# Cross-attention and feed-forward of a decoder layer as one block: one batch after the other, with the gate and up weights' codes transposed during the mixer

## The reference, cut to what matters

```python
x = x + mixer(layernorm(x))                       # scan over time, 2048 channels, 16 states, then @ W_out.T
x = x + matmul(fake_quant(layernorm(x), s1, z1), fake_quant(ctx, s2, z2))
def qlinear(x, w):                                # both sides: round(t / s) * s, s = max|row| / 127
    return einsum('bsh,oh->bso', fake_quant(x, -1), fake_quant(w, 1))
h = silu(qlinear(n, w_gate)) * qlinear(n, w_up)   # n = layernorm(x); 2752 hidden channels
x = x + qlinear(h, w_down)
```

## Time and profile before

| what | us |
|---|---|
| median of 3 runs | 1680.31 (1670.72 to 1685.57) |
| the profiled execution | 1669.6 |
| its span, first to last instruction | 1667.8 |
| PE busy | 1408.3 (84%) |
| DVE busy | 1335.1 (80%) |
| ACT busy | 929.3 (56%) |
| POOL busy | 946.3 (57%) |

### The profile page before, as it was taken

One profiled execution on the slowest core, in us unless ns is written; L12 is line 12 of the kernel. 1 busy time (PEld: TensorE's weight loads), 2 busy tenths in 40 slices (PEclk: granted clock), 3 DMA queues, 4 the chain that ended last, 5 costly groups with the idle time before them and its releaser, 6 DMA issues. The chain is left out here.

```text
span 1667.8 us, 17950 instructions
## 1 busy us (share of the span) xinstructions
PE 1408.3 (84%) x5576; PEld 727.8 (44%) x5576; DVE 1335.1 (80%) x1641; ACT 929.3 (56%) x1375; POOL 946.3 (57%) x767
## 2 busy tenths in 40 slices
PE   6999577788888987768898888888999994999898
PEld 3444344444444443444454454444434442444443
DVE  6585899999999979999999988889047556777684
ACT  1211557768768655867767767755234122556670
POOL 0000679889899878879999898897100000333300
PEclk9999788999999999877999999999999996999899
DMA  7597333443453432433683682664473103589504
GB/s 275 201 351 261 92 118 107 169 145 107 152 162 108 169 101 96 140 100 111 216 274 113 225 273 82 237 217 158 168 290 132 54 26 94 137 189 192 121 3 174
DMA packets 155468, 264.38 MB, mean 159 GB/s; under 512 B 76560, under 2 KB 94096, under 8 KB 149552
## 3 DMA queue, kind: packets, MB, share of 16 engines
q1 hardware_dynamic: 151056, 236.27, 43.9%
q10 hardware_dynamic: 4320, 27.00, 4.4%
HBM read 207.60 MB, written 38.60 MB: 148 GB/s over the span
## 5 line engine op out<-in xcount | busy, mean ns | idle before, releaser
L1093 DVE TENSOR_TENSOR_SCAN hbuf<-decay,hbuf 128x512 f32<-128x512 f32 x492 | 587.2, 1208 | 24.0 <-ACT decay L788 23.5
L788 ACT ACTIVATE decay<-delta,chan_sb 128x512 f32<-128x512 f32 x492 | 334.2, 686 | 281.9 <-DVE hbuf L1093 280.4
L598 PE MATMUL turn<-ident,hbuf 128*128 128x128 f32 x2048 | 338.2, 295 | 179.2 <-DVE hbuf L1093 128.7
L598 PEld LDWEIGHTS turn<-ident,hbuf 128*128 128x128 f32 x2048 | 255.1, 150 | 450.6 <-DVE hbuf L1093 199.6
L1107 DVE SCALAR_TENSOR_TENSOR acc<-turn,pn,acc 128x512 f32<-128x512 f32 x360 | 262.2, 728 | 41.1 <-PE turn L598 40.1
L927 POOL TENSOR_TENSOR hbuf<-wout,sx 128x512 f32<-128x512 f32 x172 | 216.0, 1289 | 15.0 <-DVE wout L1080 15.0
L927 POOL TENSOR_TENSOR hbuf<-du,sx 128x512 f32<-128x512 f32 x172 | 218.5, 1305 | 1.7 <-DMA sx<-bt_scratch 1.7
L948 POOL TENSOR_TENSOR acc<-acc,part 128x512 f32<-128x512 f32 x120 | 153.1, 1276 | 52.1 <-ACT part L798 51.0
L1796 PE MATMUL bank<-codes,wout 128*128 128x512 bf16 (+1 forms) x704 | 153.9, 382 | 1.0 <-PEq L1210 1.0
L580 PE MATMUL bank_g<-wout,codes 128*128 128x512 f32 x256 | 136.9, 622 | 0.0
L510 PE MATMUL bank_u<-wout 128*128 128x512 f32 x224 | 113.2, 625 | 3.7 <-DMA wout<-in_wu 2.8
(11 more groups left out here) (217 smaller groups left out, 2171.0 us busy)
## 6 DMA issues: line engine op xcount, KB each, us to landing
wout<-in_woutT SPq DMA_DIRECT2D x48, 512.0 KB, 4.2
sx<-bt_scratch SPq DMA_DIRECT2D x86, 256.0 KB, 3.7
codes<-in_wg SPq DMA_DIRECT2D x8, 2048.0 KB, 9.3
ubuf<-u_scratch SPq DMA_DIRECT2D x16, 1024.0 KB, 6.6
wout<-in_w_gate SPq DMA_DIRECT2D x26, 512.0 KB, 4.8
wout<-in_w_up SPq DMA_DIRECT2D x26, 512.0 KB, 4.6
raw_d<-in_w_down ACTq DMA_DIRECT2D x8, 1376.0 KB, 7.0
b_more<-bt_scratch SPq DMA_DIRECT2D x42, 256.0 KB, 3.5
```

The costliest lines, as they stand in the source:

```text
L598: last = pe.transpose(turn[t % 2][:, j * P:j * P + P], hbuf[:, s % 4, j, t * P:t * P + P], ident[:, :])
L788: act.activation(decay_place(q), delta[:, G % 2, j, :], ACT.Exp, scale=a_col(GD * (G % GROUPS) + j, n)).then_inc(dA_done, 1)
L1093: dve.tensor_tensor_scan(h, decay_place(q), h, 0.0, ALU.mult, ALU.add).then_inc(scan_done, 1)
```

## The change

`attend` and `feed_forward` become one block, `tail`, with no barrier between them.

1. In the mixer the codes of the weights are made half a unit at a time: scale, write, scale, write. SP transposes each half by a DMA into a small buffer (`turn_quant`) and then stores it in the layout that PE needs (`store_quant`). There are 88 of each in place of 44 stores. There is one buffer before and one behind the transposing DMA, so the next half waits for the last.
2. The units of the feed-forward are ordered by batch: units 0 to 21 are batch 0, 22 to 43 batch 1. Their weights are loaded plain, 512 KB a unit, and once for each batch.
3. STAGES ends with the projection. What is left of tiles 5, 6 and 7 is put between the first units, at fixed unit numbers in each engine's list.
4. PE has two pairs of banks for the units in place of four.
5. The peak and scales of batch 0 are made after unit 24, and DVE makes its codes from unit 28 on. Those of batch 1 are made during the first matmuls with w_down.
6. w_down's matmuls go by pairs of tiles: (0,1), (2,3), (4,5), then 6 and 7 alone.

```diff
-            def store_quant(u):
+            def turn_quant(h):
+                n = unit_rows(h // 2)
+                sp.wait_ge(q_step, 2 * (h + 1))
+                if h >= 1:
+                    sp.wait_ge(q_stored, 16 * h)
+                sp.dma_start(qturn[:, :, 0:n], qcode[0:n, :], transpose=True).then_inc(q_turned, 16)
+
+            def store_quant(h):
+                u, lo = h // 2, KC // 2 * (h % 2)
                 m, c, n = u % 2, u // 2, unit_rows(u)
-                sp.wait_ge(q_step, 4 * (u + 1))
-                sp.dma_start(wq_dram[m, c * P:c * P + n, :], qcode[0:n, :]).then_inc(q_stored, 16)
+                sp.wait_ge(q_turned, 16 * (h + 1))
+                sp.dma_start(wq_dram[c, :, m, lo:lo + KC // 2, 0:n], qturn[:, :, 0:n]).then_inc(q_stored, 16)
...
                     for q in (2 * s - 2, 2 * s - 1):
                         for o in (quant_at(q) if q >= 0 else ()):
+                            if o % 2 == 1:
+                                if o >= 3:
+                                    store_quant(o // 2 - 1)
+                                turn_quant(o // 2)
                             if o % 4 == 3:
-                                store_quant(o // 4)
...
                     if plain:
-                        act.wait_ge(q_step, o - 1)
-                        if u >= 1:
-                            act.wait_ge(q_stored, 16 * u)
+                        act.wait_ge(q_step, o)
+                        if o >= 3:
+                            act.wait_ge(q_turned, 16 * (o // 2))
...
-    starts = list(range(NT - 1)) + [None, NT - 1] + [None] * 3
+    STAGES = [(i if i < NT - 1 else None,) + tuple(i - lag if i >= lag else None for lag in (1, 2, 3)) for i in range(NT)]
     shared = [use for _, tb, _, td in STAGES for use in (("B", tb), ("D", td)) if use[1] is not None]
+    shared += [("D", 5), ("B", 7), ("D", 6), ("D", 7)]
...
+    WD_UNITS = [(3, 9), (12, 17)] + [(17 + 4 * i, 21 + 4 * i) for i in range(6)]
...
+    HID_AT = 28
...
+            def load_wT(u):
+                c, _, r = at(u)
+                if u >= WT:
+                    sp.wait_ge(up_mm, u - WT + 1)
+                elif u == 0:
+                    sp.wait_ge(ctx_code, 2 * KC)
+                    sp.wait_ge(x1_done, FIRST)
+                sp.dma_start(wT[:, u % WT, :, :, 0:r], wq_dram[c, :, :, :, 0:r]).then_inc(wT_load[u % WT], 16)
...
+            for u in range(UNITS):
+                products(u)
+                if u == 5:
+                    turn_code3(5)
+                if u == 6:
+                    turn_code(7)
+                if u == 7:
+                    row_sums(7)
+                    cross(7)
+                if u == 9:
+                    turn_code3(6)
+                if u == 14:
+                    turn_code3(7)
+                if u == 24:
+                    turn_peak(0, bank_p[0])
+                if u == 26:
+                    spread_ih(0, bank_p[1])
+                if u == 40:
+                    spread_sd()
+            down((0, 1), 0, 11)
+            turn_peak(1, bank[0])
+            down((0, 1), 11, 16)
+            spread_ih(1, bank[1])
+            down((0, 1), 16, OC)
+            down((2, 3), 0, OC)
+            down((4, 5), 0, OC)
+            down((6,), 0, OC)
+            down((7,), 0, OC)
...
+            for u in range(UNITS + 1):
...
+                if u < UNITS:
+                    silu(u)
+                for t, q in wd_pieces(u):
+                    round_d(t, q)
+                if u >= 1:
+                    size(u - 1)
...
+                if u == 6:
+                    keep_codes(5)
+                    affine3_of(6)
+                if u == 7:
+                    copy_codeT(7)
```

More of the change, by code:

```diff
@@ new lines, in tail @@
+        hid1 = part(20480, L * HID_OWN).rearrange("p (c t) -> p c t", t=L)
+        ih_row = [part(28160, 512), gs[0]]
+        q0 = [part(28672 + 256 * b, 256).bitcast(BF16) for b in range(BATCH)]
+        late = wout[:, OC // 2:DC, :].rearrange("p r j -> p (r j)")
+        raw_d = [late[:, 0:INTER], part(3072, INTER)]
+        code_d = late[:, 3072:3072 + OC * P // 2].bitcast(BF16)
+        peak = [late[:, 4480:4992], part(29184, 512)]
+        res = [late[:, i * H:i * H + H] for i in range(2)]
@@ L1232, in attend @@
+        chunk = [ctx_raw[0], ctx_raw[1], xn3[:, 0, :], xn3[:, 1, :]]
         ones = sb("ones", [P, P], BF16)
```

792 lines of the change are left out of this document (423 added, 369 removed).

## The result

The changed kernel is slower: 1718.56 us, the median of 4 runs (1714.25 to 1723.67), against 1675.51 of 4 runs of the kernel before, a ratio of 1.026 with a 95% interval of 1.022 to 1.030. The forecast was 1655, the range 1625 to 1690. The profiled execution took 1716.42 us with a span of 1714.6.

A forecast was written before the change was run, and what follows sets the result against it. PE was taken to bound the tail except in two holes (34.4 and 16.9 us). 1625.7 + 14 (first units) + 3 (later units) + 3 (mixer) + 1.8 gave 1647.5, ratio 0.987, hence 1655; range 1625 to 1690.

The forecast's parts named there:

- The base of the sum: Tail: PE's remaining work from 1378.7, 241.1 us, plus an end of about 5.9, gives a span of 1625.7 without new waits.
- the waits at the start of the units: First units of the tail: PE waits for DVE's scaling and ACT's copies, 14 us in all (6 to 24).
- Later units: Tail, units from 15 on: DVE is full from 28 to 43, costing 3 us (0 to 10).
- rival 1: Units 17 to 41: w_down's transposes and loads fill the DMA engines, weights land late; 16 to 40 us, about 1672; chance 0.18.
- the tail's missing gain: From the tail's first matmul to the end, a gain of about 25 us was forecast.
- The mixer: Loop: a half's transpose and store, 6.0 us one behind the other, fit into 7.7 between writes; 3 us taken (0 to 50).
- rival 2: Mixer: a half's transpose and store take 9.8 us, over 7.7 in 24 places; ACT, then DVE, lose 50 us, 1695; chance 0.13.
- the sentence after: Mixer: SP, waiting 155 us for ACT's codes already, mostly stands ready; POOL would miss B's row only after 7 us more.
- The issue: Mixer: SP's issue of a half's transpose takes 0.6 us, 88 x 0.6 = 54 us over the loop.

The follow-up runs named there:

- e10: Changed kernel with each block of w_down transposed by three DMAs, one a piece, instead of one; tail 449.7 us (changed kernel 442.0).
- e12: Changed kernel with w_down's eight transposing DMAs replaced by plain copies of the same bytes; tail 445.3 us (changed kernel 442.0).
- e5: Changed kernel with SP's list in a mixer step reordered: store, loads of w_out, then transpose; tail from 1250.2 us, span 1694.6.
- e2: Changed kernel with the transposing DMA of each half of the codes made a plain copy; ratio 1.0181 to the kernel before.
- e7: Changed kernel with the tail's loads of weights issued by ACT from unit 3 on, not SP; tail 456.0 us (changed kernel 442.0).

## Why the prediction was wrong

**The base of the sum held.** PE's work without the new waits was put at 241.1 us from the end of the projections, and the waits at the start of the units at 14. The projections end 160.9 us after the tail's first matmul (before 161.9), and the forecast's waits are there by engine and place, 3.93, 3.59, 2.25 and 2.45 us (forecast: 4.0, 5.6, 2.1 and 2), with a small one 12.6 in all. w_down's matmuls take 78.3 us (79.7 in the sum), the end 5.9 (5.9).

**Later units: the term of 3 us was too small.** DVE's later waits are the 3.1 us that it stood for. Beside them stand 11.6 us for weights, so rival 1 and the forecast were not rivals but came together, and the clock fell after two of the waits, for which the sum had nothing. The sum had 178.4 us for the units (161.4 of work, 14 and 3 of waits), and they took 196.9. Of the 35.5 us over the work, 27.3 are waits; 5.2 are the clock (6.37 us for 16 matmuls instead of 3.61, and 16.46 for 63 instead of 13.98), and 3.0 are not accounted for. The units' 18.5 us too much, less 2.4 that the projection and w_down's matmuls took below the sum, are the 16 us of the tail's missing gain. Rival 1 had the place right (units 17 to 41, w_down's transposes ahead of unit loads) and with 16 to 40 us the size too large. What stays open is how its 11.6 us divide between the queue's issue and the engines: e10 and e12 say that neither the long issue nor the transposing alone makes it.

**The mixer: the step that failed.** I put 0 to 50 us and took 3. A transpose lands in 2.5 us, a store in 3.5 (I had 3.7 and 2.3). One behind the other that is 6.0, as the sum had it, by luck: the two errors cancel, and the store of half the bytes lands later than the 2.3 us of the earlier trace rows, not sooner. 6.0 fits into 7.7. So ACT hardly waited (11.9 us), and rival 2's mechanism, ACT and then DVE losing 50 us to a slow handshake, did not happen, though its 50 us are near the 55.8 measured. What failed is the sentence after: that SP waits for ACT's codes, "so mostly it stands ready", and that only the next row of B could suffer. I had named the loads of w_out as queued behind the wait, and then priced only the row of B. A wait in SP's list holds everything behind it: 323.6 us of waits, 88 transposes of 1.19 us, and a ring of two for w_out that has to be refilled each time PE is done with a piece. The issue was at half its size as well. I had 0.6 us, from one large block divided by its squares, and that block, 3.37 us, was among the shortest of eight (median 5.25, longest 8.76). The trace of before had the price of a small one (issue in ns, minimum, median, maximum, for 8 squares):

```profile
L1752 SPq DMA_TRANSPOSE wout<-wq_scratch x38: 1232/1309/4690, 1421.9 to 1550.2; - x38
```

What should have been set side by side is 6 us of landings per half, less the time in which SP was idle anyway, and w_out's 48 loads in batch 1. I also argued from SP's idle time over the whole loop; 42.6 of the 55.8 us were lost in the part where SP had a second pacer, PE. e5 shows the mechanism with the fewest changes: the order of the list alone gives 22.5 us back.

**Issue and landing.** The Trainium skill (Advanced Engine Details and Errata, X-Bar Transpose) has transposing DMAs on trn2 as fast as regular ones. For a half of 128 KB the landings are 2.5 us transposing and 2.0 us plain (e2), so nearly; for SP the issue is 1.19 against 0.47 us, the larger difference of the two. Which of them makes the 15.9 us of e2 no run separates. The Trainium skill (DMA: Bandwidth & Descriptors, Anatomy of one DMA) has a fixed cost of about 2.0 us in each DMA that GpSimd issues, most of it until the last byte is confirmed; these are SP's, for which the section gives none. The stores of 128 KB are near it in their minimum (2.0 us) and lie above it in the median (3.5). A list in which a DMA waits for the landing of the one before pays this each time; here SP did so 87 times, for 3.7 us in the mean.

## What to carry to other kernels

A DMA queue's list is an engine like the others: when an edit puts a wait for a landing into it, go through everything that stands behind that wait, and ask which of it has a short ring and someone waiting at its end. Idle time of an issuer is no cover if it is not where the wait is. Two buffers on either side of a transfer in a chain, and the loads with the shortest ring ahead of the wait, gave back 39 of 56 us here. A second buffer behind the transfer alone gave 31, and the order alone 22, with ACT then waiting 49 us. And where two limits lie as close together as DVE and the loads in batch 1, an experiment that removes one only renames the wait.

## What the runs showed of the hardware

- Issuing a transposing DMA from SBUF to SBUF takes SP 1.19 us for 4 squares of 128 (bf16), 1.25 us for 8 (e10, median) and 3.3 us at the least for 22. Four squares and eight cost nearly the same, so a large part is fixed there. A plain copy takes 0.47 us for 128 KB (e2) and for 704 KB (e12).
- The same issue took up to 9.5 us (e7: 11.5) with other transfers under way, the plain copy never over 0.53. In the changed kernel the longest three (9.5, 7.7 and 7.5 us) lie in stretches with a DMA share of 0.77 to 0.91, the shortest two (3.4 and 3.3) in stretches of 0.57 and 0.56. No run sets the load on the DMA engines by itself.
- A 704 KB plain copy from SBUF to SBUF beside the units lands in 9.3 us in the median (e12), the transposing one in 8.8; at the least it is 3.4 against 5.2. So beside the units the median landing was no longer for the transposition.
- Word for word the same tail took 442.0 to 448.4 us in eight kernels, with the granted clock of some stretches at 0.76 or 0.88 in one and 1.00 in another.
